# Row norms of the second self-attention: reciprocal roots as a power on GpSimd instead of a square root on ScalarE

## The reference, cut to what matters

```python
for l in range(L):                        # L = 2
    x = x + _attn(_ln(x, ln1_w[l], ln1_b[l]), wq[l], wk[l], wv[l], wo[l], ...)   # 16 heads of 8
    h = _ln(x, ln2_w[l], ln2_b[l])
    x = x + (_token_moe if l % 2 == 0 else _seq_moe)(h, ...)

def _ln(x, w, b):
    m = x.mean(-1, keepdims=True)
    v = x.var(-1, keepdims=True)
    return (x - m) / jnp.sqrt(v + 1e-05) * w + b
```

## Time and profile before

| | |
|---|---|
| median of 3 runs | 1197.53 us (1196.03 to 1198.46) |
| the profiled execution | 1198.17 us |
| its span, first to last instruction | 1196.5 us |
| busy: TensorE, VectorE, ScalarE, GpSimd | 987.8, 824.7, 729.6, 581.7 us |
| mean granted TensorE clock | 0.876 of full speed |

### The profile page before, as it was taken

One profiled execution on the slowest core, in us unless ns is written; L12 is line 12 of the kernel. 1 busy time (PEld: TensorE's weight loads), 2 busy tenths in 40 slices (PEclk: granted clock), 3 DMA queues, 4 the chain that ended last, 5 costly groups with the idle time before them and its releaser, 6 DMA issues.

```text
span 1196.5 us, 30533 instructions
## 1 busy us (share of the span) xinstructions
PE 987.8 (83%) x9835; PEld 762.4 (64%) x9835; DVE 824.7 (69%) x1992; ACT 729.6 (61%) x1831; POOL 581.7 (49%) x781
## 2 busy tenths in 40 slices
PE   3999989999986689999479998847999989899403
PEld 2677766677756679999446666636777769355201
DVE  4599999899965846666479998674222254699873
ACT  2577777888862037777359889735555513688543
POOL 6355545555560035555489996404334300588333
PEclk9799999999995569999769999958999975799855
DMA  4000040000002012222110004000000010011002
GB/s 128 10 16 13 15 148 2 2 1 0 0 1 71 0 27 66 66 66 65 45 34 25 27 26 133 18 1 1 0 0 0 0 55 25 21 45 46 23 0 70
DMA packets 51921, 38.77 MB, mean 32 GB/s; under 512 B 6072, under 2 KB 45476, under 8 KB 51860
## 3 DMA queue, kind: packets, MB, share of 16 engines
q1 hardware_dynamic: 46956, 28.88, 8.3%
q0 software_dynamic: 4320, 8.86, 2.9%
q10 hardware_dynamic: 584, 0.26, 0.1%
HBM read 29.13 MB, written 8.85 MB: 32 GB/s over the span
## 4 chain that ended last, share of the span: by engine, by line
PE 45%; ACT 15%; DVE 11%; issue 11%; POOLq 7%; POOL 4%; DVEq 3%; DMA 2%; SPq 1%; ACTq 0%
PE ps_s L1056 9%; PE ps_t L1140 7%; PE ps_o L1056 7%; PE ps_v L1056 6%; PE ps_a L1056 5%; POOLq L728 5%; PE ps_t L1056 4%; ACT work L851 3%; DVEq L1664 2%; POOL work L729 2%; ACT vst L842 2%; ACT xcts L817 1%; ACT probs_t L859 1%; POOLq L718 1%; PE ps_v L1160 1%
## 5 line engine op out<-in xcount | busy, mean ns | idle before, releaser
L664 POOL TENSOR_TENSOR kbd<-kts,kmask 128x512 f32<-128x512 f32 x192 | 240.5, 1275 | 173.8 <-ACT qts L835 84.2
L692 POOL DMA_INDIRECT xg<-x_rows,row_from x71 | 73.6, 1036 | 137.9 <-DVE slot_of L1657 70.1
L859 ACT COPY probs_t<-ps_t 128x1024 f32<-128x1024 f32 x96 | 97.2, 1013 | 66.2 <-PE ps_t L1140 66.2
L1492 DVE TENSOR_REDUCE rowmax<-ps_s 128x16 f32<-128x1024 f32 x96 | 116.8, 1217 | 20.5 <-PE ps_s L1056 19.7
L1056 PE MATMUL ps_s<-kbd,qts 64*64 64x512 f32 (+1 forms) x1024 | 124.8, 559 | 0.0
L1495 DVE TENSOR_TENSOR work<-ps_s,rowmax 128x1024 f32<-128x1024 f32 x96 | 117.6, 1225 | 3.3
L1140 PE MATMUL ps_t<-ident,work 128*128 128x128 f32 x768 | 105.1, 281 | 15.2 <-ACT work L851 13.8
L1056 PE MATMUL ps_o<-vst,probs_t 128*64 128x18 f32 x3072 | 107.7, 213 | 7.6 <-ACT probs_t L859 7.6
L1056 PEld LDWEIGHTS ps_o<-vst,probs_t 128*64 128x64 f32 x3072 | 98.1, 138 | 20.2 <-ACT probs_t L859 10.0
L1140 PEld LDWEIGHTS ps_t<-ident,work 128*128 128x128 f32 x768 | 87.7, 144 | 23.7 <-ACT work L851 23.6
L851 ACT ACTIVATE work<-work 128x1024 f32<-128x1024 f32 x96 | 100.9, 1051 | 1.4 <-DVE work L1495 1.2
(11 more groups left out here) (378 smaller groups left out, 2378.0 us busy)
## 6 DMA issues: line engine op xcount, KB each, us to landing
y_rows<-work SPq DMA_DIRECT2D x71, 64.0 KB, 1.6
w<-in_L_ffn_e_w_dram SPq DMA_DIRECT2D x2, 2048.0 KB, 8.6
ctx_dup<-in_ctx_dram SPq DMA_DIRECT2D x64, 64.0 KB, 2.3
x_res<-in_x_dram SPq DMA_DIRECT2D x4, 512.0 KB, 6.6
ctx_in<-in_ctx_dram SPq DMA_DIRECT2D x32, 64.0 KB, 1.8
x_rows<-h_all SPq DMA_DIRECT2D x1, 2048.0 KB, 9.2
work<-in_ctx_dram SPq DMA_DIRECT2D x8, 256.0 KB, 2.9
out_dram<-work SPq DMA_DIRECT2D x16, 128.0 KB, 1.8
```

Source lines behind the costliest of these rows:

```text
L664: i = pool.tensor_tensor(km[:, par, g, :, :], kts[:, par, g:g + 1, :].to_broadcast([P, 8, SEQ]), kmask[:, :, :], ALU.mult)
L692: pool.indirect_dma_start(xg[:, t % XBUFS, :], None, x_d, bass.IndirectOffsetOnAxis(row_from[:, t:t + 1], 0)).then_inc(xg_loaded[t % XBUFS ...
L859: nc.scalar.copy(probs_t[:, par, :], ps_t[:, :]).then_inc(S["pts_ready"], 1)
L1492: V.tensor_reduce(rowmax[:, par, :], s3, AXX, ALU.max).then_inc(S["max_ready"], 1)
```

## The change

The eight group roots leave ScalarE. VectorE now writes variance + eps of a group into `vares` behind the statistics of the group's last tile (its `fetched_stats`), and GpSimd raises it to the power -0.5 with a tensor_tensor against a constant tile `minus_half` (128x4), straight into `rstd`. The step has a lag of GROUP + 1 = 5 turns and is last in GpSimd's turn. VectorE's reciprocal of the group and its wait fall away; `eps_col` goes, and the counts of `vare_ready` and `rstd_ready` in the later norms are shifted to fit.

```diff
-        eps_col = sb("eps_col", [P, 1])
+        minus_half = sb("minus_half", [P, GROUP])
...
-                fresh(pool.memset(eps_col[:, :], EPS))
+                fresh(pool.memset(minus_half[:, :], -0.5))
...
-            straight([(AHEAD, kbd_after_scores), (AHEAD - 1, four_biases), (0, fetch)])
+            def group_root(t, par):
+
+                if t % GROUP == 0:
+                    pool.wait_ge(S["vare_ready"], CH_SELF1 + t // GROUP + 1)
+                    pool.tensor_tensor(rstd[:, t:t + GROUP], vares[:, 0, t:t + GROUP], minus_half[:, :], ALU.pow
+                                       ).then_inc(S["std_ready"], 1)
+
+            straight([(AHEAD, kbd_after_scores), (AHEAD - 1, four_biases), (0, fetch), (GROUP + 1, group_root)])
...
-                act.wait_ge(S["vare_ready"], k + 1 - (NGROUP if k >= CH_PRE1 else 0))
+                act.wait_ge(S["vare_ready"], k + 1)
...
-            def group_root(t, par):
-
-                if t % GROUP == 0:
-                    act.wait_ge(S["stats_done"], t + GROUP)
-                    nc.scalar.activation(stds[:, 0, t:t + GROUP], aggr[:, t:t + GROUP, 1], ACT.Sqrt, bias=eps_col[:, :]
-                                         ).then_inc(S["std_ready"], 1)
-
-            straight([(0, group_root)] + [step for step in attention(1, 1) if step] + [(0, normalise)])
+            straight([step for step in attention(1, 1) if step] + [(0, normalise)])
...
-                dve.wait_ge(S["rstd_ready"], k + 1)
+                dve.wait_ge(S["rstd_ready"], k + 1 - (NGROUP if k >= CH_PRE1 else 0))
...
                 V.bn_aggr(aggr[:, t, :], stats[:, t, :]).then_inc(S["stats_done"], 1)
+                if t % GROUP == GROUP - 1:
+                    c = slice(t + 1 - GROUP, t + 1)
+                    dve.wait_ge(S["stats_done"], t + 1)
+                    V.tensor_scalar(vares[:, 0, c], aggr[:, c, 1], EPS, None, ALU.add).then_inc(S["vare_ready"], 1)
...
                     dve.wait_ge(S["std_ready"], CH_SELF1 + g + 1)
-                    V.reciprocal(rstd[:, c], stds[:, 0, c]).then_inc(S["rstd_ready"], 1)
-                    dve.wait_ge(S["rstd_ready"], CH_SELF1 + g + 1)
```

## The result

| | before | after |
|---|---|---|
| median | 1196.07 us (6 runs, 1194.66 to 1198.46) | 1204.54 us (6 runs, 1203.18 to 1207.43) |
| profiled execution, span | 1198.17, 1196.5 us | 1203.43, 1201.6 us |
| one group while fetches run | 20.90 us | 22.00 us |
| ScalarE busy, GpSimd busy in all | 729.6, 581.7 us | 712.6, 590.6 us |

The ratio is 1.0072, 95% interval 1.0054 to 1.0090: the change makes this kernel slower, by 8.5 us between the medians and 5.3 us between the profiled executions. The forecast was no measurable change, +0.9 us (1198.4, range 1193.5 to 1204.0). All ratios leave out three slow runs of the experiments (one of the first experiment's kernel, 1260.1 us, two of the kernel before beside it, 1220.8 and 1222.7); the medians are of all runs.

The account below looks back on a forecast made before the run. GpSimd's queue (20.87 us a group) was taken to set the pace up to the last fetch, tied with the table-load loop (20.88). Six roots at 0.5 us minus 2.12 gave +0.9 us: 1198.4 us, range 1193.5 to 1204.0.

Parts of the forecast that it names:

- c: Price of one group's root as a power on GpSimd, 128x4: taken as 0.5 us, between 0.22 and 1.05.
- Rival C: GpSimd: the power is dear and six roots count in full; 1201.7 us at 1.05 us each; chance 0.31.
- Rival D: GpSimd: the power's first use is slow once, before the first keys; 5 us stall gives 1203.4 us; chance 0.04.
- 6c - 2.12: Whole change in us: six roots counting in GpSimd's queue, minus one pair of table loads; +0.9 at c = 0.5.
- The second root: In the ramp: its delay of GpSimd's keys is taken up by their 0.58 us wait for TensorE, so adds nothing.
- The pair of loads behind the last fetch: ScalarE's table loads around the root after GpSimd's last fetch: their removal saves 2.12 us.
- Keys 0: GpSimd's first block-diagonal keys in the second self-attention: start at 606.36 + c, delayed by the first root.
- the cover over the later first root: Ramp: first root some 2 us later, hidden because keys wait for GpSimd's queue anyway, over 2 us to spare.
- The equal bounds: Second self-attention, per four-tile group: GpSimd's queue needs 20.87 us, TensorE and ScalarE's loop with table loads 20.88.
- Rival B: ScalarE's table loads were the bound, GpSimd only followed: six pairs gone, 12.7 us faster, 1184.8 us; chance 0.18.
- The wait for eps: GpSimd's power waiting for VectorE's eps addition: over in time behind the fetches, zero cost.
- VectorE's collision: GpSimd's power holding up VectorE through shared SBUF interfaces: zero in the sum, about zero even at worst.

Follow-up runs that it names:

- the first experiment: Kernel before with the root left out: VectorE writes variance + eps into rstd, no Sqrt loads on ScalarE, no power on GpSimd; 1208.33 us, ratio 0.9972.
- the sizes run: Kernel before plus eight GpSimd powers and multiplies of 1, 4, 16 and 64 columns in idle time behind the last keys; the longest took 10.54 us.
- fetches out: Kernel before and changed kernel, each without the 64 indirect fetches of the second self-attention: 1183.20 us (ratio 0.9754) and 1174.27 us (0.9683).

## Why the prediction was wrong

**What the power costs was the step that failed**: "I take c = 0.5, the geometric middle". It is 1.05 us, in the queue 1.10. The sentence behind the choice, "but on 4 columns only", held the mistake: the function costs 0.16 us a column beside the fixed part, and four columns of it are already 0.64 us (the sizes run). The middle lay between a multiply, which the operation isn't, and a fetch, with which it has only the length in common. Rival C named mechanism and price and had 0.31; its 1201.7 was the better forecast. Rival D did not occur: the first power took 1.06 us, like the others.

**The sum's form held, with one slip.** "6c - 2.12": the term 6c came out as 1.72 + 5.50 = 7.22. Five groups gave 5 x 1.10 exactly. The second root was said to be taken up by the 0.58 us that keys 3 waited for TensorE; that is true for c up to 0.58 and not beyond. Better is 7c - 0.58 = 7.12. The price stood in the sum twice, once in the term and once in whether its cover was enough, and the cover wasn't worked out anew at the upper end. With c = 1.10 the corrected sum is 7.12 - 2.12 = +5.0; the parts that it covers came to +5.18. That the spans differ by nearly the same, 5.1, is luck: -1.45 in front of the stage, +1.14 of clock and +0.23 behind it cancel.

**The pair of loads behind the last fetch** was put at -2.12 and gave -2.04.

**Clock and ramp.** Keys 0 came at 606.03 (forecast 606.36 + c, from a stage that began 1.45 us earlier), so the cover over the later first root held. The lower granted clock at the stage's end cost 1.14 us, a little more than the 1 us allowed, which was meant for the ramp. That the change caused it isn't shown, and the later profiles speak against it.

**The equal bounds** were right: GpSimd's queue at 20.87 (the group grew by exactly the added piece) and the loop with the loads at 20.8 (fetches out). Rival B is refuted for the kernel as it is. Its price of 2.12 us a group was wrong too: only 1.08 was to be had. TensorE's wait for y, from 640 to 715 us, is 11.4 us with the loads and 16.0 without them (both without fetches), so a part of what ScalarE gave back became a wait for VectorE.

**Costs put at zero.** The wait for eps was over in time in seven of eight roots, as said. VectorE's collision was not where I looked, at the power, but beside the keys: VectorE's nbias now comes while the keys run (700.20 to 702.69) and is held until they end:

```profile
701.12 1.59 DVE L1745 SCALAR_TENSOR_TENSOR nbias<-aggr,rstds 128x4 f32<-128x4 f32 x1
```

Over its eight executions its median is 1.58 us, where it was 0.41. VectorE's busy time in the group is 21.38 of 21.97 us, 1.8 more than before: nbias took 1.1 more, and the four first combines (L1681) 0.25 more each beside the keys (rows can overlap a little). By the Trainium skill, "GPSIMD Engine Reference", section "Key points", the two engines share their SBUF interfaces and collide over instructions with two SBUF inputs; nbias and the key multiply are such a pair, and the trace agrees. The group still grew by the queue's own 1.10 and no more.

**What stays open.** Of the 8.5 us between the medians the profiled executions explain 5.3; the changed kernel ran three times at 1203.2 to 1203.4 and three times at 1205.7 to 1207.4, beside the kernel before at 1196.0 to 1198.5 and then 1194.7 to 1196.1. So the difference was 5.9 us and then 11.3, and the second three left no trace. Why TensorE's completions reach the others late on three chips and did not in the first comparison is not settled either. On chip 3 the change is worth -3.9 us (1208.28 against 1212.19) in place of +8.5; that GpSimd's queue has slack there is seen in the changed kernel's trace, but the kernel before has no trace on that chip.

## What to carry to other kernels

An operation that no row shows deserves no middle between bounds: ask how its cost grows with size, and forecast from the end whose mechanism is like it. Where a wait is said to cover a cost, write the cover into the sum as max(0, cost - cover) and evaluate it at both ends of the range. Two bounds that are equal to 0.1% mean that work moved from one to the other counts in full and work removed from one counts for nothing; taking out what keeps one of them busy shows both, and the third behind them, in one pair of runs.

## What the runs showed of the hardware

- A power of two tensors on GpSimd: 0.59 us at 128x1, 1.00 to 1.05 at 128x4, 10.54 at 128x64; a multiply is 0.20, 0.21 and 0.31.
- An indirect fetch occupies GpSimd for 0.94 to 0.99 us (medians of the two, longest 1.05) and leaves a gap of 0.30 in front of the second; a plain transfer of the same rows costs it 0.57 and 0.55 (means over 32 each) and no gap.
- While indirect fetches run, VectorE sat idle for outputs of TensorE that by the trace had ended, up to 1.7 us in the unchanged kernel (2.1 in the one with four powers), in traces of three chips and there in up to all four tiles of a group; GpSimd's keys waited 0.6 to 0.9 us at a time in the unchanged and the changed kernel. The unchanged kernel's groups are 22.2 to 24 us there instead of 20.9. With plain transfers or none such waits don't occur. The stages behind this one last 414.6 to 417.9 us in every trace.
- A VectorE instruction with two inputs in SBUF (nbias, 128x4) took 0.16 us at 598.52, with no GpSimd multiply beside it, and 1.59 at 701.12, inside one.
